# Moving register loads and a stage's weight loads in a two-layer transformer kernel

## The reference

```python
h = _layernorm(x) * (1 + ca) + sa
x = x + ga * _L0_attn_ref(h, ...)
h = _layernorm(x) * (1 + cb) + sb
x = x + gb * _L0_ffn_ref(h, ...)      # experts
...
h = _layernorm(x) * (1 + ca) + sa
x = x + ga * _L1_attn_ref(h, Wq, bq, Wkv, bkv, Wo, bo)
h = _layernorm(x) * (1 + cb) + sb
x = x + gb * _L1_ffn_ref(h, ...)

def _L0_ffn_ref(...):                 # after routing
    order = argsort(flat_e); xs = x[order // TOP_K]
    gu = ragged_dot(xs, gate_up_proj, group_sizes)
    gate, up = split(gu, 2)
    y = ragged_dot(silu(gate) * up, down_proj, group_sizes)
    out = zeros.at[tok].add(y * w)
```

## Time and profile before

| | us |
|---|---|
| median of three runs (lowest, highest) | 2276.95 (2269.54, 2277.73) |
| the profiled execution: its own time | 2271.91 |
| its span in the trace | 2270.1 |
| PE busy / DVE / ACT / POOL | 2031.7 / 1026.1 / 742.7 / 735.3 |
| expert stage, about | 388 to 1275 |
| second attention, about | 1275 to 1680 |

### The profile page before, as it was taken

One profiled execution on the slowest core, in us unless ns is written; L12 is line 12 of the kernel. 1 busy time (PEld: TensorE's weight loads), 2 busy tenths in 40 slices (PEclk: granted clock), 3 DMA queues, 4 the chain that ended last, 5 costly groups with the idle time before them and its releaser, 6 DMA issues. The chain is left out here.

```text
span 2270.1 us, 38924 instructions
## 1 busy us (share of the span) xinstructions
PE 2031.7 (89%) x11188; PEld 1319.8 (58%) x11189; DVE 1026.1 (45%) x3238; ACT 742.7 (33%) x1747; POOL 735.3 (32%) x668
## 2 busy tenths in 40 slices
PE   4799867999999999999999369999958999999998
PEld 2676643555555555555555146666536878878787
DVE  2367668234556322222222166676624444443432
ACT  0233227222222222222222046776733333322322
POOL 1244310444545444444444253544311102011000
PEclk8799879999999999999999679999988999999999
DMA  7222432687777778888886401100011121121210
GB/s 242 89 73 86 166 104 93 152 208 187 185 176 187 178 178 196 199 204 186 186 210 145 121 32 32 33 22 14 1 48 47 65 75 65 66 74 65 77 64 27
DMA packets 107128, 258.55 MB, mean 114 GB/s; under 512 B 25488, under 2 KB 29200, under 8 KB 106896
## 3 DMA queue, kind: packets, MB, share of 16 engines
q1 hardware_dynamic: 68240, 163.61, 22.5%
q0 software_dynamic: 35552, 88.63, 19.9%
q10 hardware_dynamic: 3232, 4.95, 0.6%
HBM read 196.55 MB, written 59.54 MB: 113 GB/s over the span
## 5 line engine op out<-in xcount | busy, mean ns | idle before, releaser
L1209 PE MATMUL bank<-arena 128*128 x1272 | 452.0, 499 | 29.5 <-issue 26.9
L1209 PEld LDWEIGHTS bank<-arena 128*128 128x128 f32 x1272 | 229.5, 190 | 187.3 <-issue 59.7
L1226 PE MATMUL bank<-arena 96*128 x632 | 299.9, 597 | 4.9 <-issue 4.3
L1164 POOL DMA_INDIRECT x_sum<-arena x158 | 253.6, 1605 | 86.0 <-issue 65.5
L1175 POOL DMA_INDIRECT arena<-h_moe,arena x158 | 156.7, 992 | 376.7 <-DVE arena L1319 371.5
L1311 DVE SCALAR_TENSOR_TENSOR arena<-arena,bank 128x192 f32<-128x192 f32 x159 | 66.0, 415 | 345.5 <-ACT arena L1245 343.3
L1921 PE MATMUL bank<-x_hi,w_hi 128*128 128x512 f32 x512 | 200.8, 392 | 6.0 <-DVE x_lo L2054 6.0
L1921 PE MATMUL bank<-x_hi,w_lo 128*128 128x512 f32 x512 | 199.4, 389 | 0.0
L1921 PE MATMUL bank<-x_lo,w_hi 128*128 128x512 f32 x512 | 199.2, 389 | 0.0
L1245 ACT ACTIVATE arena<-bank 128x192 f32<-128x192 f32 x159 | 52.8, 332 | 415.2 <-PE bank L1209 380.3
L1226 PEld LDWEIGHTS bank<-arena 96*128 96x128 f32 x632 | 107.2, 190 | 86.3 <-issue 86.2
(11 more groups left out here) (329 smaller groups left out, 3439.8 us busy)
## 6 DMA issues: line engine op xcount, KB each, us to landing
arena<-in_moe_up SPq DMA_DIRECT2D x64, 768.0 KB, 8.3
ffn_arena<-in_ffn_up SPq DMA_DIRECT2D x64, 512.0 KB, 3.3
arena<-in_moe_down SPq DMA_DIRECT2D x64, 384.0 KB, 8.9
arena<-in_L_wmod SPq DMA_DIRECT2D x12, 1024.0 KB, 6.7
x_sum<-route SPq DMA_DIRECT2D x18, 256.0 KB, 2.9
x_res<-in_L_attn_x SPq DMA_DIRECT2D x1, 4096.0 KB, 18.3
h_moe<-arena SPq DMA_DIRECT2D x16, 256.0 KB, 2.1
x_sum<-x_res SPq DMA_DIRECT2D x16, 256.0 KB, 2.4
```

What stands on the lines that cost most here:

```text
L1164: nc.gpsimd.indirect_dma_start(out=x_sum[b], out_offset=bass.IndirectOffsetOnAxis(ap=st_dst[:, b], axis=0), in_=y[:, b], in_offset=None, c ...
L1209: mm = nc.tensor.matmul(psum[2 + b][:, 0:2 * FI], xgT[:, b, k], up_ring[:, bass.ds((e % RING) * UPW + k * 2 * FI, 2 * FI)], start=(k == 0) ...
L1226: mm = nc.tensor.matmul(psum[6 + b][:], hiddenT[:, b, n], down_ring[:, bass.ds((e % RING) * DOWNW + n * C, C)], start=(n == 0), stop=(n == 1))
```

## The change

Three edits.

1. In the expert loop the register load of `g` on PE and that of `after` on DVE move to the heads of their turns. PE's second load (`before`) stays.
2. The 11 transfers of the second attention's weights are issued by SP at the head of the expert stage, behind the load of expert 3, into a part of `arena` above `TAIL`; the expert stage's `y` moves to `route` to make room. The scaling and the selection matrices are made by DVE behind its expert loop, after a wait for all 11. The second attention loses the waits on them and `weights_ready`.
3. The second attention brings four row tiles ahead instead of two.

```diff
@@ expert stage, SP
                 load(AHEAD, AHEAD)
+                wo_rows = a["L1_attn_Wo"].rearrange("(c r d) n -> c d r n", c=NKV1, r=HP)
+                for c in range(NKV1):
+                    sp.dma_start(later1.wo[HD * c:HD * c + HD], wo_rows[c]).then_inc(late_in, 16)
+                sp.dma_start(later1.bo, a["L1_attn_bo"].partition_broadcast(P)).then_inc(late_in, 16)
+                sp.dma_start(later1.wq[:], a["L1_attn_Wq"].rearrange("(k p) n -> p k n", p=P)).then_inc(late_in, 16)
...
                 landed(32 * E // RING, RING - 1)
+                sp.wait_ge(late_in, 16 * N_LATE)
@@ expert stage, PE
                 def turn(before, g, after):
+                    if g is not None:
+                        e_g = pe.value_load(tile_expert[0:1, bass.ds(g[0], 1)], min_val=0, max_val=E - 1)
                     if before is not None:
...
                         t, b, _ = g
-                        e = pe.value_load(tile_expert[0:1, bass.ds(t, 1)], min_val=0, max_val=E - 1)
+                        e = e_g
@@ expert stage, DVE
                 def turn(before, g, after):
+                    if after is not None:
+                        e = dve.value_load(tile_expert[0:1, bass.ds(after[0], 1)], min_val=0, max_val=E - 1)
                     if g is not None:
...
                     if after is not None:
                         t, b, half = after
-                        e = dve.value_load(tile_expert[0:1, bass.ds(t, 1)], min_val=0, max_val=E - 1)
...
                 schedule(dve, turn, sure=sure)
+                wo, bo = later1.wo, later1.bo
+                dve.wait_ge(late_in, 16 * N_LATE)
+                st.did(tt(wo[:], wo[:], mod[:, 1, 2].unsqueeze(1).to_broadcast([P, HP, C]), ALU.mult))
+                st.did(tt(bo, bo, mod[:, 1, 2], ALU.mult))
+                st.did(nc.vector.tensor_copy(later1.sel..., ident...))
+                st.did(nc.vector.tensor_copy(later1.spread..., ident...))
+                st.settle()
@@ second attention
-            XB = 8
+            XB, ROWS_AHEAD = 8, 4
...
-                rows_in(0)
-                rows_in(1)
-                sp.dma_start(wq[:], ...).then_inc(w_in, 16)
...
+                for t in range(ROWS_AHEAD):
+                    rows_in(t)
@@ second attention, PE
-                        pe.wait_ge(w_in, 16 * N_DMA)
                         pe.wait_ge(hT_out, p + 1)
@@ second attention, DVE
                     if f == 0:
-                        weights_ready()
                         meta_values()
```

More of the change, by code:

```diff
@@ L175, in __call__, with __init__ @@
                 return v
+        NHEAD = C // HD
+        NQK = NHEAD + NKV1
+        HM = P // META
+        class Later:
+            def __init__(self):
+                cv = Carver(TAIL)
+                self.wq, self.wkv, self.wo = cv(KC, C), cv(KC, 2 * NKV1 * HD), cv(HP, C)
+                self.bqk_row, self.bv_row, self.bo = cv(NQK * HD), cv(NKV1 * HD), cv(C)
+                self.meta_head = cv(HM)
+                self.sel, self.spread = cv(HP, P)[0:NHEAD], cv(P)[0:META]
         class Routed:
@@ L1106, in adaln_two_layers @@
             w_read, slots_known, rows_known = psem("m_w_read"), psem("m_slots_known"), psem("m_rows_known")
+            late_in = psem("m_late_in")
+            N_LATE = 11
             def schedule(eng, turn, steps=None, per=0, sure=None):
@@ L1346, in _ @@
                 schedule(dve, turn, sure=sure)
+                wo, bo = later1.wo, later1.bo
+                dve.wait_ge(late_in, 16 * N_LATE)
+                st.did(tt(wo[:], wo[:], mod[:, 1, 2].unsqueeze(1).to_broadcast([P, HP, C]), ALU.mult))
+                st.did(tt(bo, bo, mod[:, 1, 2], ALU.mult))
+                st.did(nc.vector.tensor_copy(later1.sel.rearrange("n r (c d) -> n r c d", c=NKV1),
+                                             ident[0:NHEAD, 0:NHEAD].rearrange("n (c r) -> n r c", r=HP).unsqueeze(3).to_broadcast([NHEAD, HP, NKV1, HD])))
+                st.did(nc.vector.tensor_copy(later1.spread.rearrange("p (h k) -> p h k", h=HM),
+                                             ident[0:META, 0:META].unsqueeze(1).to_broadcast([META, HM, META])))
+                st.settle()
         with ExitStack() as ph, nc.Block() as block:
             psem = phase_semaphores(ph)
-            NHEAD = C // HD
-            NQK = NHEAD + NKV1
             VRING, GROUPS = 5, 6
+            wq, wkv, wo, bo = later1.wq, later1.wkv, later1.wo, later1.bo
+            bqk_row, bv_row, meta_head, sel, spread = later1.bqk_row, later1.bv_row, later1.meta_head, later1.sel, later1.spread
             cv = Carver()
-            wq, wkv, wo = cv(KC, C), cv(KC, 2 * NKV1 * HD), cv(HP, C)
-            bqk_row, bv_row, bo = cv(NQK * HD), cv(NKV1 * HD), cv(C)
             rope = cv(2, 4, HD)
@@ L1367, in adaln_two_layers @@
             v = cv(VRING, NKV1, HD)
-            HM = P // META
             v_meta = cv(2, HP, 2, HD)
-            meta_head = cv(HM)
-            spread = cv(P)[0:META]
             prob = cv(GROUPS, HP, KEYS1)
@@ L1387, in adaln_two_layers @@
             h = down_scale[:]
-            XB = 8
+            XB, ROWS_AHEAD = 8, 4
             xb = route[:].rearrange("p (b c) -> p b c", b=XB)
-            names = ("w_in", "ready", "x_sums", "stats", "rstd", "xhat", "h_done", "hT_mm", "hT_out", "q_mm", "q_rows", "kv_mm",
+            names = ("ready", "x_sums", "stats", "rstd", "xhat", "h_done", "hT_mm", "hT_out", "q_mm", "q_rows", "kv_mm",
                      "kv_rows", "roped_q", "roped", "qT_mm", "q_in", "kx_done", "kT_mm", "k_in", "s_mm", "mx_done", "meta_sub",
                      "exp_done", "meta_exp", "r_done", "rb_out", "pT_mm", "pT_out", "pM_mm", "pM_out", "o_mm", "o_out", "wo_mm", "x_pre", "x_out",
-                     "spread_done", "meta_mm", "v_meta_done", "dve_steps", "pool_steps")
-            (w_in, ready, x_sums, stats, rstd, xhat, h_done, hT_mm, hT_out, q_mm, q_rows, kv_mm,
+                     "meta_mm", "v_meta_done", "dve_steps", "pool_steps")
+            (ready, x_sums, stats, rstd, xhat, h_done, hT_mm, hT_out, q_mm, q_rows, kv_mm,
              kv_rows, roped_q, roped, qT_mm, q_in, kx_done, kT_mm, k_in, s_mm, mx_done, meta_sub,
              exp_done, meta_exp, r_done, rb_out, pT_mm, pT_out, pM_mm, pM_out, o_mm, o_out, wo_mm, x_pre, x_out,
-             spread_done, meta_mm, v_meta_done, dve_steps, pool_steps) = (psem("b_" + n) for n in names)
+             meta_mm, v_meta_done, dve_steps, pool_steps) = (psem("b_" + n) for n in names)
             x_in = [psem(f"b_x_in{b}") for b in range(XB)]
@@ L1433, in rows_in @@
                     sp.dma_start(xb[:, t % XB], x_sum[1][t * P:(t + 1) * P]).then_inc(x_in[t % XB], 16)
-                rows_in(0)
-                rows_in(1)
-                sp.dma_start(wq[:], a["L1_attn_Wq"].rearrange("(k p) n -> p k n", p=P)).then_inc(w_in, 16)
-                sp.dma_start(wkv[:], a["L1_attn_Wkv"].rearrange("(k p) n -> p k n", p=P)).then_inc(w_in, 16)
-                sp.dma_start(bqk_row[:, 0:C], a["L1_attn_bq"].partition_broadcast(P)).then_inc(w_in, 16)
-                sp.dma_start(bqk_row[:, C:], a["L1_attn_bkv"][0:NKV1 * HD].partition_broadcast(P)).then_inc(w_in, 16)
-                sp.dma_start(bv_row, a["L1_attn_bkv"][NKV1 * HD:].partition_broadcast(P)).then_inc(w_in, 16)
-                wo_rows = a["L1_attn_Wo"].rearrange("(c r d) n -> c d r n", c=NKV1, r=HP)
-                for c in range(NKV1):
-                    sp.dma_start(wo[HD * c:HD * c + HD], wo_rows[c]).then_inc(w_in, 16)
-                sp.dma_start(bo, a["L1_attn_bo"].partition_broadcast(P)).then_inc(w_in, 16)
-                sp.dma_start(meta_head, a["meta_head"]).then_inc(w_in, 16)
+                for t in range(ROWS_AHEAD):
+                    rows_in(t)
                 tables = a["rope"].rearrange("(t p) k d -> t p k d", p=P)
@@ L1485, in turn @@
                     if w is not None:
-                        pool.wait_ge(ready, 2)
                         pool.wait_ge(xhat, w + 1)
```

31 lines of the change are left out of this document (12 added, 19 removed).

## The result

The changed kernel takes 2212.78 us in the median of four runs (2206.72 to 2214.35), against 2274.36 (2269.54 to 2277.73) for the kernel before on the same chip, now with a fourth run beside the three of the first table: a ratio of 0.9726, 95% interval 0.9698 to 0.9754, so 62 us less. The profiled execution has a span of 2211.1 us for 2270.1, 59.0 less. The forecast was 2225, in a range of 2208 to 2254.

The account below looks back on a forecast made before the run. The prediction took PE's own instruction stream in the expert stage as the bound. Its terms, -48 - 5 + 13 + 3 + 1 + 0 - 11.8 = -47.8 us, took 2271.91 to 2224.1, given as 2225, range 2208 to 2254.

Parts of the forecast that it names:

- PE's register load: Expert loop: moved ahead of the wait for hidden, the load hides behind the down products; -48 and -5 us.
- Stall and shorter group: Expert loop, gate/up products: PE's whole stall ahead of them goes, -48 us; their group shortens after an unstalled start, -5.
- Late gathers: Expert loop: shorter turns leave gathers less time, 30 turns wait for rows instead of 18; +13 us.
- The balance of the gather's lead: Expert loop, gather issue to use: shorter turns take 2 x 0.34 us, DVE's moved load returns about 0.5; net 0.2 less.
- gathers take the place: Rival, expert loop: nearly every expert load makes a turn late, losing 35 us instead of 13; 2246 us, chance 0.18.
- DVE's register load: Expert loop, ahead of hidden: DVE's wait for ACT mostly covers the load, thinly in matrix-transform turns; +3 us.
- The 11 transfers: Head of the expert stage: 3.2 MB beside the first gathers delays them little; +1 us, bounds 0 and +15.
- The scaling at the end: End of the expert stage: four DVE instructions take about 3.5 us and end just under POOL's drain; 0 us.
- The attention's first turns: Second attention's start: first projection no longer waits for weights, -9.4 us, and POOL's steps shorten, -2.4; together -11.8.
- The slower rival: Expert loop: PE's load at the head begins only after the last down product, exposed each turn; 2356 us, chance 0.04.
- The stall isn't the load: Rival, expert loop: PE's stall has another cause, such as the wait for expert weights; only the seam gains, about 2261, chance 0.10.

Follow-up runs that it names:

- e4: Kernel before, register loads in place, with POOL filling 1024 unused columns between gather and scatter, about 1 us a turn: 2270.88 us, 0.9984.
- e1: Kernel before with only PE's register load of g moved to the head of the turn in the expert loop: 2262.22 us, 0.9950 of the kernel before.
- e11: Changed kernel with an unused 512-column DVE multiplication ahead of the signal that lets POOL gather: 2252.49 us, 0.9912 of the kernel before.
- e12: Changed kernel with an unused 512-column DVE multiplication behind the signal that lets POOL gather: 2214.49 us, 0.9734 of the kernel before.
- e6: Changed kernel with the 11 transfers issued behind the loads of experts 4 to 7: 2210.23 us, 0.9710 of the kernel before.
- e3: Changed kernel with both register loads back at their old places, leaving only the seam's edits: 2269.82 us, 0.9979 of the kernel before.
- e10: Like e9, with DVE's two small copies also moved ahead of the product hidden: 2195.53 us, 0.9659 of the kernel before.
- e9: Changed kernel with PE's second load ahead of the row transposes, 11 transfers behind experts 4 to 7, two row tiles ahead: 2198.24 us, 0.9675.

## Why the prediction was right, and where it was not

**PE's register load.** Stall and shorter group were put at -48 - 5 = -53; measured -43.4 - 9.5 = -52.9. That the sum fits to 0.1 us is luck: the stall gave 4.6 us less and the group 4.5 more. The mechanism was right, with one thing more: the load isn't only covered, it no longer meets the scatter's moment, so it is 303 ns. 13 of its 158 loads in the loop are still over 0.4 us, all of them 2 to 3 us after a scatter. `e4` settles the question that was left open, whether the loads are long by their moment: with the scatter moved and the loads in place, the median fell from 644 to 303 ns.

**Late gathers.** Put at +13, with 30 late turns for 18. Measured: 12 late turns, 8.4 us of waits for 8.5, and -3.2 + 2.2 = -1.0 us in the intervals behind them. Late turns also lengthen the interval ahead of the transposes of the rows, by 3.9 us for 1.4 over the usual turn, which stands inside the -9.5 above; counted here, the term is +1.5 and the shorter group -12, the bound that was given for it. Either way this is the term that was mis-sized, by 12 to 14 us, and most of the difference between 2225 and 2213. The balance of the gather's lead was the right one: 2 x 0.34 us are taken, and what DVE's load gives back was put at 0.5 of its 0.73. It gives back all of it (issue 1.98 us after the transposes for 2.72), so the median lead is 8.00 us for 8.09, not 0.2 less. The step that failed is to work with the mean: late turns come from the shortest leads. 61 of DVE's loads were over 0.4 us before and 4 are now, 44 gathers were issued more than 3 us after the transposes and none is now, and 27 of 155 leads were under 7.5 us for 5 now. What was not seen either is how much hangs on the moment of the issue: with PE's load moved alone (`e1`), and with the gather held for 0.7 us (`e11`), 40 us and more are lost. The rival "gathers take the place" was no rival in the changed kernel, but it is what PE's half of the change meets without DVE's.

**DVE's register load.** Put at +3. Nothing of it is seen: its median is 305 ns; the interval ahead of the transposes of hidden, where a late `hidden` would show, is 274.6 us in the changed kernel as in `e1`, which has not this move; and `e12` shows that 0.69 us more on DVE, behind the signal, cost nothing. The Trainium skill gives a `tensor_load` a floor of about 600 ns ("DMA: Bandwidth & Descriptors", "Latency and other measured facts"). No trace here agrees: both engines have 0.30, except behind a scatter.

**The 11 transfers.** Put at +1, measured +5.4, in the bounds. The argument was taken from loads in the middle of the loop, where gathers have 8 us of lead; the first gathers have none, PE waits for them at once, and every microsecond of sharing shows. The same page of the Trainium skill says that a DMA engine goes round between its queues packet by packet ("Queues, rings and completion order"). By that rule the term was to be 0.8 to 1.6. `e6`, the run with the transfers moved away, has 4.9 us less of this wait, and over all traces it is 12.6 to 13.6 us in the six kernels with the transfers at the stage's head and 8.2 to 9.0 in the other eight. So a backlog of another queue costs a transfer on which somebody waits already more than that reading of the rule allowed.

**The scaling at the end.** Put at 0, with 3.5 us for the four instructions. They took 3.4 (1221.48 to 1224.84) and ended 0.6 us ahead of POOL's drain.

**The attention's first turns.** Put at -11.8, measured -10.2. The wait for the weights is gone as forecast: the first projection comes 7.8 us earlier counted from SP's first transfer, and 9.4 earlier counted from the addition of the first row tile. POOL's step that stood beside `weights_ready` now takes 1.26 us for 3.19:

```profile
1249.22 1.26 POOL L1503 TENSOR_TENSOR arena<-arena,mod 128x512 f32<-128x512 f32 x1
```

Two things were not in the sum. One is that the first row tile is added 4.8 us after SP's first transfer for 3.3, and 4.5 to 5.0 in every kernel with the seam's edits, with two tiles ahead as with four. In `e3` the first transfer has landed 2.8 us after SP began, for 2.6 before, but the second, which goes to `route`, 4.7 for 3.2; why it takes longer stays open. The other is that the first projection takes 6.03 us for 5.14, at a lower granted clock. Stretches around it, before and after (columns as in the earlier trace rows):

```profile
1295.00:1302.00 7.00, 5.52 (x10) 2.40 (x11) 1.13 (x2) 0.00 (x0) 0.29 (x1) 0.74 0.20 71
```

```profile
1239.00:1246.00 7.00, 6.14 (x9) 2.49 (x9) 0.85 (x2) 0.03 (x1) 0.01 (x1) 0.66 0.00 0
```

0.66 for 0.74 as a mean, and over the projection alone, 1239.08 to 1245.11 and 1295.70 to 1300.84, 0.61 for 0.72. So it spends 4.7 us at the 1.2 GHz level before the clock rises to 2.4, where it spent 2.9.

The slower rival (the load waits for the products ahead of it) is refuted by the timeline: no gap in nearly all turns. "The stall isn't the load" is refuted by `e4`, where shorter loads at the old place took 31.7 us off the stall.

## What to carry to other kernels

Removing a stall in a loop shortens the time that every prefetch has: before removing it, work out the lead of each transfer in unstalled turns, look at the shortest leads and not at the median, and make the edit that restores the lead together with it; tested one by one, both may look worthless. Put a register load ahead of any wait that can be late, not behind it, since it can hide only behind work already queued. A transfer that somebody waits for at once should have no bulk transfers issued beside it; moved in among the loop's own loads, they cost it half of what the move had saved (`e6`).

## What the runs showed of the hardware

- A register load from on-chip memory takes 0.30 us on PE and on DVE, but up to 1.14 us when it starts 1.75 to 3.25 us after an indirect scatter (with addition) starts on POOL: 590 of 625 loads between 2 and 2.75 us were over 0.4 us, none of 1940 before 1.75. Why is open.
- POOL's drain at the end of the expert stage took 4.64 us, to the nanosecond the same in both kernels, and ended last there.
- Gathers of 128 rows landed 3.3 to 8.7 us after their issue, 5.7 in the median, with the DMA engines at 0.83 of their time (the changed kernel, the two at the stage's head left out). Issued 0.5 us earlier (`e10` against `e9`) they landed 0.5 us later after the issue.
